# Delta-rule layers: a tile of 32 tokens of each of four images in place of 128 tokens of one

## What is computed

```python
def delta_rule(q, k, v, beta):
    def step(W, inp):
        qt, kt, vt, bt = inp
        wk = jnp.einsum('bhde,bhe->bhd', W, kt)
        v_new = bt * (vt - wk)
        W = W + jnp.einsum('bhd,bhe->bhde', v_new, kt)
        out = jnp.einsum('bhde,bhe->bhd', W, qt)
        return (W, out)
    _, outs = jax.lax.scan(step, W0, (q, k, v, beta))
    return outs

qkvb = jnp.einsum('sbi,oi->sbo', h, slow_w).reshape(slen, bsz, H, 3 * D + 1)
q, k, v, beta = jnp.split(qkvb, [D, 2 * D, 3 * D], axis=-1)
q = jax.nn.softmax(q, axis=-1); k = jax.nn.softmax(k, axis=-1); beta = jax.nn.sigmoid(beta)
```

## Time and profile before

| | us |
|---|---|
| three runs | 5322.65, 5342.67, 5358.6 (median 5342.67) |
| span of the profiled execution | 5373.4 |
| first delta-rule stage in it | 331.5 to 1235.0 |
| second delta-rule stage in it | 1614.3 to 2470.0 |
| TensorE busy over the whole span | 4530.5 (84%) |
| VectorE, ScalarE, GpSimd busy | 2972.1 (55%), 2152.0 (40%), 831.7 (15%) |

### The profile page before, as it was taken

How to read it: one execution, slowest core, us unless ns; L and a number is a source line. 1 busy time by engine, 2 the same in 40 slices (tenths; PEclk the granted TensorE clock), 3 DMA queues, 4 the chain that set the end, 5 groups by cost and what they waited for, 6 DMA issues and landing times. The chain is left out here.

```text
span 5373.4 us, 139944 instructions
## 1 busy us (share of the span) xinstructions
PE 4530.5 (84%) x57100; PEld 2834.8 (53%) x57101; DVE 2972.1 (55%) x5849; ACT 2152.0 (40%) x4091; POOL 831.7 (15%) x2139
## 2 busy tenths in 40 slices
PE   3679898887997888897688886799999999984995
PEld 1237777773436777774355554354454545433663
DVE  3444444453024544454488886488686877852343
ACT  1133223232123333331466664277575766721221
POOL 0000000000000000000355553011111111104012
PEclk7788878798998988898899998899999999985997
DMA  1000000000000000000100000000000000006123
GB/s 42 2 7 3 3 3 3 3 3 18 0 0 9 4 3 3 3 4 3 38 1 1 1 1 0 10 1 1 1 0 1 0 1 1 0 3 217 61 84 101
DMA packets 47552, 85.70 MB, mean 16 GB/s; under 512 B 7121, under 2 KB 38129, under 8 KB 46065
## 3 DMA queue, kind: packets, MB, share of 16 engines
q1 hardware_dynamic: 40944, 61.84, 3.3%
q0 software_dynamic: 6144, 16.79, 1.0%
HBM read 45.05 MB, written 33.55 MB: 15 GB/s over the span
## 5 line engine op out<-in xcount | busy, mean ns | idle before, releaser
L1775 PE MATMUL psum<-hm_ex,hm_mix 128*128 128x512 f32 x1024 | 510.4, 621 | 42.3 <-ACT hm_Aq L1855 38.3
L1841 ACT ACTIVATE hm_ex<-psum,hm_nm 128x1024 f32<-128x1024 f32 x256 | 285.6, 1116 | 299.4 <-DVE hm_nm L1899 299.4
L1775 PEld LDWEIGHTS psum<-hm_ex,hm_mix 128*128 128x128 f32 x1024 | 175.6, 191 | 352.5 <-issue 344.8
L1914 DVE COPY hm_A<-psum 128x1024 f32<-128x1024 f32 x256 | 312.9, 1222 | 51.5 <-PE psum L1784 47.9
L1909 DVE TENSOR_SCALAR_CACHE_REDUCE hm_plus<-hm_Aq,hm_cbcol,hm_sums 128x1024 f32<-128x1024 f32 x256 | 340.5, 1330 | 0.0
L1899 DVE TENSOR_REDUCE hm_nm<-psum 128x1 f32<-128x1024 f32 x256 | 311.0, 1215 | 13.5 <-PE psum L1763 13.5
L1784 PEld LDWEIGHTS psum<-K,hm_Aq 128*128 128x128 f32 x2048 | 236.6, 140 | 150.0 <-issue 145.4
L957 DVE TENSOR_TENSOR fw_M<-fw_M,psum 128x256 f32<-128x256 f32 x256 | 107.8, 421 | 348.1 <-PE psum L728 345.6
L1846 ACT ACTIVATE hm_junk<-hm_Aq 128x1024 f32<-128x1024 f32 x256 | 270.6, 1057 | 30.3
L1763 PE MATMUL psum<-hm_kt,hm_qd 64*32 64x512 f32 x4096 | 280.1, 606 | 0.0
L1321 ACT ACTIVATE pt_signs<-pt_acts,pt_tb 128x1024 f32<-128x1024 f32 (+1 forms) x224 | 227.6, 1018 | 116.1 <-POOL pt_tb L1188 95.0
(11 more groups left out here) (379 smaller groups left out, 9044.6 us busy)
## 6 DMA issues: line engine op xcount, KB each, us to landing
ex_rows_in<-ex_zero SPq DMA_DIRECT2D x2, 5120.0 KB, 24.8
ex_xs<-ex_rows_in SPq DMA_DIRECT2D x80, 128.0 KB
ex_rows_out<-ex_ys SPq DMA_DIRECT2D x80, 128.0 KB, 1.7
ex_w<-in_ex_w SPq DMA_DIRECT2D x2, 4096.0 KB
X<-in_x SPq DMA_DIRECT2D x2, 2048.0 KB, 12.5
out_y<-X SPq DMA_DIRECT2D x2, 2048.0 KB, 9.0
ff_w<-in_ff_w SPq DMA_DIRECT2D x2, 1024.0 KB, 5.8
pt_w_proc<-in_pt_proc SPq DMA_DIRECT2D x1, 2048.0 KB, 7.6
```

What stands on the lines that cost most here:

```text
L1775: mm = pe.matmul(bank[4 + c], mix[:, u, :], ex[:, u, 512 * c:512 * c + 512], start=True, stop=True)
L1841: act.activation(ex[:, u, :], flat2(psum[:, 2 * u:2 * u + 2, :]), ACT.Exp, bias=nm[:, u:u + 1], accum_out=rsum[:, u:u + 1]).then_inc(s_ex, 1)
L1914: dve.tensor_copy(A[:, :, :, QT_ * t:QT_ * t + QT_], flat2(psum[:, 6:8, :]).rearrange("p (m g n) -> p m g n", m=MT, g=HEADS)).then_inc(s_a ...
```

## The change

A tile becomes 32 tokens of each of the four images: 128 rows again, but its four blocks belong to four images. The four states are independent, so one tile needs one state step instead of four in a row, and no state is reset in the middle.

- The state `M` is now compact: for each image and head its 32x32 block, without the zeros beside it. `through_state` becomes 32 products of 32x32 (two halves of 16, L732 of the new kernel), `read_state` 32 (L721), and `new_state` 64 in two halves: in turn one for the change of the state (L744) and one for what the queries see inside the block (L747), from the compact masked product `qm`. `intra`, its spread, `keep` and `inside` are gone.
- VectorE has one `corrected` and one `state` a tile, each over all 128 rows. ScalarE copies the output out in two pieces.
- The pipeline has four steps: gram matrices and masks for tile i, factors and first solve for v = i - 1, the other three solves for s = i - 2, the state step for r = i - 3. `ntx` is kept twice and `qm` four times. The factors of the solution are still spread to 128x128, and `solve` is what it was. The projection is split in two pieces, at two places of the list.
- GpSimd fetches the first tile ahead of its zero fills. The loop has seven rounds of four bodies; four bodies stand ahead of it and three behind.

```diff
...
+        qm = sb("qm", [P, 4, HEADS, DH])
+        z3x, ntx = sb("z3x", [P, HEADS, P]), sb("ntx", [P, 2, HEADS, P])
...
-        intra = sb("intra", [P, 4, HEADS, P])
-        keep = sb("keep", [P, NT])
-        M = sb("M", [P, 2, P])
...
+        pu = sb("pu", [P, 2, HEADS, DH]); pk = sb("pk", [P, C]); pkt = sb("pkt", [P, 2, C])
+        U = sb("U", [P, HEADS, DH])
+        M = sb("M", [P, 2, 2, 2, DH])
...
+        place = lambda g, j: 4 * (j % 2) + 2 * g + j // 2
+        tokens = lambda i: H[:, :, :].rearrange("p h (b n) -> p h b n", b=B)[:, :, :, bass.ds(i * LEN, LEN)]
...
         def bodies(body, eng, start=None):

-            for i in range(-1, 4):
-                body(i, i % 4, i + 1 < NT, i >= 0, i >= 1, i >= 2)
-            with eng.Fori(1, NT // 4 - 1) as j:
+            for i in range(4):
+                body(i, i, True, i >= 1, i >= 2, i >= 3)
+            with eng.Fori(1, NT // 4) as j:
                 if start:
...
                     body(j * 4 + a, a, True, True, True, True)
             if start:
                 start()
-            for i in range(NT - 4, NT + 2):
-                body(i, i % 4, i + 1 < NT, i < NT, i - 1 < NT, True)
+            for i in range(NT, NT + 3):
+                body(i, i % 4, False, i < NT + 1, i < NT + 2, True)
...
+                def fetch(i):
+                    pool.tensor_copy(stage[:, :, :].rearrange("p h (b n) -> p h b n", b=B), tokens(i)).then_inc(s_staged, 1)
...
-
-                for to in (z3x, ntx):
-                    pool.memset(to[:, :, :], 0.0).then_inc(s_zero, 1)
-                for a in range(4):
-                    pool.memset(intra[:, a, :, :], 0.0).then_inc(s_zero, 1)
-                bodies(body, pool)
+                    if new and not (isinstance(i, int) and i + 1 >= NT):
+                        pool.wait_ge(s_pj1, i + 1)
+                        fetch(i + 1)
+
+                fetch(0)
+                pool.memset(z3x[:, :, :], 0.0).then_inc(s_zero, 1)
+                for a in range(2):
+                    pool.memset(ntx[:, a, :, :], 0.0).then_inc(s_zero, 1)
...
-                def project(i):
-                    pe.wait_ge(s_staged, i + 1)
-                    for b, (lo, hi) in ((0, (0, QKN)), (1, (QKN, 3 * C + HEADS))):
-                        for h in range(CH):
-                            mm = pe.matmul(bank[b][:, 0:hi - lo], stage[:, h, :], w[:, h, lo:hi],
-                                           start=(h == 0), stop=(h == CH - 1))
-                    mm.then_inc(s_proj, 1)
+                def project(i, n, lo, hi, sig):
+                    for h in range(CH):
+                        mm = pe.matmul(bank[n][:, 0:hi - lo], stage[:, h, :], w[:, h, lo:hi],
+                                       start=(h == 0), stop=(h == CH - 1))
+                    mm.then_inc(sig, 1)
...
-                def through_state(a, c):
+                def read_state(a):
+
+                    for c in range(B):
+                        for g in range(2):
+                            for j in range(4):
+                                at = 256 + 64 * (c // 2) + 32 * g
+                                mm = pe.matmul(bank[6 + c % 2][rows(j), at:at + 32], M[rows(j), c % 2, c // 2, g, :],
+                                               tr[rows(j), a, 1, g, rows(c)], start=(c < 2 and g == 0), stop=False)
+                    mm.then_inc(s_o, 1)
+
+                def through_state(a, half):
+
                     for g in range(2):
-                        at = slice(P * g + 32 * c, P * g + 32 * c + 32)
-                        mm = pe.matmul(bank[6][rows(c), P * g:P * g + P], pkt[:, a % 2, at], M[:, g, :],
-                                       start=True, stop=True)
+                        for c in range(B):
+                            for jb in range(2):
+                                j = 2 * half + jb
+                                at = 32 * (2 * g + half)
+                                mm = pe.matmul(bank[6 + jb][rows(c), at:at + 32],
+                                               pkt[rows(j), a % 2, P * g + 32 * c:P * g + 32 * c + 32],
+                                               M[rows(j), c % 2, c // 2, g, :], start=True, stop=True)
                     mm.then_inc(s_ra, 1)

-                def with_state(a, c):
-
-                    for g in range(2):
-                        for j in range(4):
-                            pe.matmul(bank[7][rows(j), P * g + 32 * c:P * g + 32 * c + 32], M[rows(j), g, rows(j)],
-                                      tr[rows(j), a, 1, g, rows(c)], start=(c == 0 and g == 0), stop=False)
-                    for g in range(2):
-                        for j in range(4):
-                            at = P * g + 32 * j
-                            mm = pe.matmul(bank[6][rows(j), C + at:C + at + 32], kk[rows(c), a, at:at + 32],
-                                           U[rows(c), at:at + 32], start=True, stop=True)
-                    mm.then_inc(s_rm, 1)
...
-                def inside(a):
-                    for g in range(2):
-                        for j in range(HG):
-                            hd = HG * g + j
-                            mm = pe.matmul(bank[7][rows(j), P * g:P * g + P], U[:, DH * hd:DH * hd + DH],
-                                           intra[:, a, 4 * (hd % 2) + hd // 2, :], start=False, stop=(g == 1))
-                    mm.then_inc(s_intra, 1)
...
+                def new_state(a, half):
+
+                    for c in (2 * half, 2 * half + 1):
+                        for g in range(2):
+                            for j in range(4):
+                                at = 64 * half + 32 * g
+                                n = place(g, j)
+                                pe.matmul(bank[6 + c % 2][rows(j), 128 + at:160 + at],
+                                          kk[rows(c), a, P * g + 32 * j:P * g + 32 * j + 32], U[rows(c), n, :],
+                                          start=False, stop=False)
+                                mm = pe.matmul(bank[6 + c % 2][rows(j), 256 + at:288 + at], U[rows(c), n, :],
+                                               qm[rows(c), a, n, :], start=False, stop=(half == 1 and g == 1))
+                    mm.then_inc(s_ui, 1)
+
+                def body(i, a, new, inv, sol, rec):
...
+                    if rec:
                         pe.wait_ge(s_ptc, r + 1)
-                        pe.wait_ge(s_m, r * 5 + 1)
+                        pe.wait_ge(s_m, r + 1)
+                        if since(i, 4):
+                            pe.wait_ge(s_fin, r)
+                        pe.sem_inc(s_go, 1)
                         through_state(ra, 0)
-                    if so:
-                        pe.wait_ge(s_zx, s + 1)
-                        solve(z3x, given, s_y)
-                    if ch:
+                    if sol:
+                        pe.wait_ge(s_nt, s + 1)
+                        pe.wait_ge(s_r0, s + 1)
+                        solve(by, first, s_ap)
...
+                    if rec:
+                        pe.wait_ge(s_u, r + 1)
+                        pe.sem_inc(s_go, 1)
+                        read_state(ra)
+                    if inv:
+                        pe.wait_ge(s_z, v * 2 + 1)
+                        pe.sem_inc(s_go, 1)
+                        product(z2, l2)
+                    if sol:
+                        pe.wait_ge(s_rk, s * 2 + 2)
+                        solve(by, later, s_ap)
+                    if rec:
+                        pe.wait_ge(s_o, r + 1)
+                        pe.wait_ge(s_qm, r + 1)
+                        pe.sem_inc(s_go, 1)
+                        new_state(ra, 0)
+                    if inv:
+                        pe.wait_ge(s_tt, v + 1)
+                        pe.sem_inc(s_go, 1)
+                        product(tt, l2)
+                    if rec:
+                        pe.wait_ge(s_ui, r * 2 + 1)
+                        pe.sem_inc(s_go, 1)
+                        new_state(ra, 1)
...
+                        act.activation(pkt[:, a % 2, :], bank[2][:, 0:C], ACT.Copy).then_inc(s_ptc, 1)
+                    if rec:
+                        act.wait_ge(s_m, r + 2)
+                        to = tokens(r).rearrange("p g (s b) t -> p b s g t", b=2)
+                        for c in range(2):
+                            last = act.activation(to[:, c], bank[6 + c][:, 256:384].rearrange("p (s g t) -> p s g t", s=2, g=2),
+                                                  ACT.Copy)
+                        last.then_inc(s_fin, 1)
+                    if inv:
+                        act.wait_ge(s_t, v * 5 + 5)
+                        if since(i, 3):
+                            act.wait_ge(s_ap, v * 3 - 3)
+                        spread(ntx[:, (a - 1) % 2], bank[5][:, 0:C].rearrange("p (h j) -> p h j", j=DH), -1.0, s_nt)
+                        act.wait_ge(s_y, v + 1)
+                        if since(i, 2):
+                            act.wait_ge(s_pu, v)
```

(21 more changed lines are left out.)

## The result

The changed kernel takes 5391 us (median) against 5347 of the kernel before: ratio 1.0103, interval 1.0070 to 1.0136, so 1% slower. The forecast was the same sign and 165 us; measured are 44.

The account below looks back on a forecast made before the run. TensorE's queue, paced by code loading, bounds: bodies of 25.2 us at full and 34.1 at half clock (share 0.55) average 29.4; with loop returns +169 us, with ends +165, from 5342.67 to about 5507 us; range 5250 to 5700.

Parts of the forecast that it names:

- What bounds the kernel: Both delta-rule stages: TensorE's in-order queue is the bound, stopping for code about every 250 matmul and load records.
- The price of a block: TensorE's quick stretches: each 16 KB code block takes 4.35 us stop to stop; 5.77 blocks a body take 25.1 us.
- The body at half clock: One body of the changed kernel with TensorE at half clock: 34.1 us, with code loading hidden under the work.
- The share of half clock: Time TensorE's clock is halved in the delta-rule stages: 0.55, taken between 0.34 and 0.86; 24 to 34% before.
- What lowers the clock: TensorE in the second half of a body: 5.5 us of code stops must raise the time at half clock.
- Loading paces, but the clock does not fall further: Rival for both layers: code stops spread thinly, half-clock share 0.10 to 0.35, time 5281 to 5345 us; chance 0.25.
- The loop's return: End of each round of four bodies: TensorE stops 3.8 us; six returns a stage instead of five, 23 us.
- Code loading is hidden after all: Rival for TensorE's small products: no code stops, body 19.7 us at full clock, time 5063 us; chance 0.13.
- cover: Work on TensorE hides the one state step, 5.1 us between new state and next use; late waits taken as 0.
- products that share a place: New-state products alternating on one 32x32 array part: at worst 1.5 us a body, 94 us uncovered; taken as 0.
- TensorE's busy share down: Sign of being right, both delta-rule stages: TensorE busy for a smaller share while VectorE and ScalarE wait for it.
- The start: Beginning of each delta-rule stage: first tile fetched ahead of POOL's zero fills shortens the 9.48 us wait, 2 us a stage.

## Why the prediction was off

- **What bounds the kernel: right.** TensorE stops for code every 250 records, and more so after the change. Half a block more or less moved the layers by 117 and 155 us, against 47 by work (69 at half clock), and the instruction queue moved the 0.77 packet more a body that was counted.
- **The price of a block: the step that failed.** "At the 4.35 us of the two stop-to-stop rows, 5.77 blocks take 25.1 us." The changed kernel's stop-to-stop rows are 3.84 and 3.94 us, the median of 67 is 3.85, and in the four bodies at full clock throughout blocks take 3.35 to 4.05. Such a body takes 21.0 to 22.2 us where I forecast 25.2. With 22.0 in place of 25.2, and 0.55 half clock, the sum gives 27.3 us a body in place of 29.4, 134 us less in both layers. The 4.35 was not misread: the kernel before has no block between two stops under 4.25. But it did not carry over to blocks of another make-up, and in that kernel itself it fell to 3.78 with small products added. What makes the old blocks longer stays open; width alone does not, since blocks with a whole solve (16 wide records) take 3.95 (median of 22) in the changed kernel. The blocks of 3.56 and 3.51 us in the earlier trace rows I set aside as ones with a head start; they were nearer.
- **The body at half clock: right, as far as is shown.** Forecast 34.1 us, by the fit 34.2.
- **The share of half clock: right in size, by luck.** Forecast 0.55, measured 0.52; the difference is worth some 23 us. The reason for it did not hold, as the next point says.
- **What lowers the clock: wrong.** I put it down to idle time in the stops. Thin products that fill most of the same time leave the clock at 0.75, wide ones bring it to 0.85 and 0.83. What exactly lowers it stays open. "Loading paces, but the clock does not fall further" named 5281 to 5345 and came out wrong as well: the clock did fall. The Trainium skill, "TensorE: Matmul & The Clock Gate", on which that rival leaned (Why this matters for your kernels), has long gaps between bursts take the clock down; the run with thin products shows it down with most of the gaps filled.
- **The loop's return: too small.** 3.8 us in the sum, 5.8 to 8.6 by the versions without loops, of which the stops make 3.1 to 3.9 in the first layer and 5.6 to 6.2 in the second. Over twelve returns that is 24 to 47 us more than I counted for the changed kernel. My check of the parts against the kernel before, 1,760 against 1,759, had the same 3.8 in it, so that it came out so close was in part luck. The Trainium skill, "Runtime: NRT & Kernel Launch" (Instruction fetch mechanics), says that a taken branch breaks the loading ahead and, where its target is not among the two blocks at hand, forces a load of it; the stop at each return and the two packets more agree.
- **"Code loading is hidden after all", 5063:** falls. The sentence of the Trainium skill, "Runtime: NRT & Kernel Launch" (Instruction fetch mechanics) that a crossing is mostly hidden does not hold for blocks of small products: 105 us of "issue" at L744 and L747.
- **VectorE, ScalarE, cover, products that share a place: right.** 3.0 us less VectorE a body; the waits on the correction and the turned tiles are 1.4 and 8.1 us in both layers; taking L744 and L747 apart gains nothing.
- **TensorE's busy share down: wrong.** It is 87% of the first stage before and after, and 87 and 86% of the second: with the clock lower, less work takes as long.
- **The start:** the first projection is now released by the weights, as foreseen, 8.09 us behind the stage before it where it was 9.48:

```profile
333.75 4.87 PE L675 MATMUL psum<-fw_w,fw_stage 128*128 128x512 f32 x8 [8.09 <-DMA fw_w<-in_slow]
```

- **Packets:** 23 for four bodies were forecast; the four bodies from 1696 on moved

```profile
q8 instruction: 25, 0.41, 1.6%
```

with a return of the loop among them, whose reloading I had not counted.

Put together: with 22.0 and 34.1 us and 0.52 a body takes 1/(0.48/22.0 + 0.52/34.1) = 27.0 us, 64 of them 1727 us, and twelve returns of 5.8 to 7.7 us make it 1796 to 1819; the profiled execution has 1824.0. So the forecast for the layers (+165) missed the runs' 44 us, or the stages' 62, because the body at full clock was 134 us too dear and the share of half clock 23, while the returns were 24 to 47 too cheap. What is left is within the scatter of executions.

## What to carry to other kernels

Where an engine's instructions are short, count them as well as their time: here a block of 256 instructions took TensorE 3.35 us or more from stop to stop, 3.85 in the median, so 48 products of 23 ns that replaced fewer, longer ones were paid as code. Do not carry the price of two blocks over to blocks of another make-up: add products of the planned shape to the kernel as it is, read by nobody, and time the blocks there (here 3.74 us in place of 4.35). Where small products stand together, wide work among them, even useless work, can be worth more than it costs (here it was in the changed kernel, and not in the one before), and these short loops with long bodies were worth writing out.

## What the runs showed that I had not expected

- 195 us of wide products that nobody reads made the kernel 70 us faster (5391 to 5322); thin ones of the same duration made it slower (5465).
- Half clock in a block that is paced by code costs next to nothing (3.94 us at half, 3.84 at full); it is paid where the next solves and projection stand, 7.10 us in place of some 3.9.
- A return of the loop cost 5.8 to 8.6 us, and in the second layer TensorE stops twice at each.
- The same solves, moved between small products, went from 292 to 329 ns a record.
